# A two-layer transformer block on one core: routed experts as tiles of sorted rows instead of every expert for every token

## The chip, the cores and the metric

The kernel runs on one core of a Trainium2 chip. The metric is the time of one execution on the device, in microseconds (us); less is better. Three runs of the kernel before were taken.

## The reference, cut to what matters

There are 8 batches of 512 tokens with 128 channels. Layer 0 is attention over the heads of a token plus a gated feed-forward of width 384, both on a layer norm of x. Layer 1 normalizes again and adds two branches: a state-space mixer with a scan over the tokens, and a mixture of 8 routed experts, of which each token uses two, plus one shared expert.

```python
xn = _layernorm(x)
x = x + _L0_attn_ref(xn, ...) + _L0_ffn_ref(xn, ...)
xn = _layernorm(x)
x = x + _L1_attn_ref(xn, ...) + _L1_ffn_ref(xn, ...)

# the scan of L1_attn: 256 channels x 16 states, over 512 tokens
hst = dA * hst + dBu;  y = jnp.einsum('bdn,bn->bd', hst, C_t)

# L1_ffn
gates = jax.nn.sigmoid(xf @ Wg)
vals, idx = jax.lax.top_k(gates, 2)
vals = vals / vals.sum(axis=-1, keepdims=True)
shared = jax.nn.silu(xf @ Ws1) * (xf @ Ws3) @ Ws2
h = jax.nn.silu(jnp.einsum('td,edf->tef', xf, We1)) * jnp.einsum('td,edf->tef', xf, We3)
routed = jnp.einsum('tef,efd,te->td', h, We2, w)
out = (shared + routed) / 3
```

## The kernel before, in words

Two blocks follow each other, `layer0` and `layer1`. Every engine has its own instruction stream, written out by hand, and semaphores (objects of the class `Count`) are the only tie between streams. An engine runs its stream in order, so an instruction that waits holds up all that stands behind it. The DRAM tensor `layer0_out` carries x from one block to the other.

**Layer 0** is a loop written out over `b` from 1 to 9. In one turn an engine works on batch `b` (`new`) and finishes batch `b - 1` (`old`). VectorE's stream of one turn is: score products (`score_prod`, L517, four of 128 x 2048), the rotary steps of batch b + 1 (`rope_q`, `rope_k`), sixteen value products (L541), maximum, three `hidden` steps, `statistics` and `normalize` of batch b + 2 (`bn_stats` L474, `bn_aggr` L479, `xn` L489), a reciprocal (L560), and `add_up` (L565), which makes x1 of batch b - 1. GpSimd does the two rest steps of the exponentials (L371, L377) and `root` (L367). SyncE's queue repeats q through DRAM, stacks the parts of the exponentials and stores x1.

**Layer 1** handles one batch in 32 **slots**, `k` from 0 to 31 (`GROUPS`), one for each group of 128 (channel, state) pairs. In the middle, two batches at a time are the body of a loop with registers (`Fori`); the first and the last batch and the tail are written out. In every slot stands the same recurrence over the engines:

- TensorE, `spread_dt` (L1578, tile `p_decay`) waits until the scan of slot k - 2 is done, then `spread_du` (L1583, tile `p_du`) until the `inject` of slot k - 1 is done.
- ScalarE, `decay` (L1178), an exponential in place on `p_decay`.
- VectorE, `inject` (L1421, tile `dbu`), then `scan` of slot k - 1 (L1427, tile `hs`).
- GpSimd, `times_c` of slot k - 1 (L1078, tile `hc`); every fourth slot TensorE sums eight passes of it in `gather_y` (L1592).

```python
pe.wait_ge(scanned.sem, scanned.at(b, k - ND + 1) if k >= ND else scanned.at(b - 1, GROUPS - ND + k + 1))
nc.tensor.matmul(p_decay[:, k % ND], spread[:, i], block_in[:, 0, s, j], start=True, stop=True).then_inc(dt_full.sem, 1)
```

Around this recurrence two other things are placed by slot number. The first is the preparation of the next batch: layer norm and RMS norm (`statistics`, `normalize`, `normalize_rms`), transposes (`turn_x`), `in_proj` (L1540), a convolution of four taps on VectorE (`convolve`, L1328 and L1331), `x_proj`, `dt_proj`, the softplus steps (L1337 to L1346), the split of the result into three bf16 parts (L1351, L1356), and `routing`, 15 small VectorE steps (L1370 to L1403) that rank the gates.

The second is the mixture of experts. It has `UNITS` = 18 **units** per batch, two for each of the eight routed experts and the shared one; the list `unit_slot` gives each unit its slot, from 4 on, and `units(b, p, k, ahead, ...)` yields those that are due. A unit is one half (128 rows) of an expert's hidden width, for all 512 tokens: TensorE `gate` three slots ahead (L1598, tile `p_g`), ScalarE a copy, a tanh and `add_one` (L1185, L1186, L1190), GpSimd `silu` (L1090, tile `sg`), TensorE `up` (L1609, tile `p_u`), VectorE `hidden` (L1440, tile `y_hid`), TensorE `down` (L1616), added up in `p_acc`. For each expert TensorE also spreads its weight per token (`spread_weight`, L1571) and VectorE multiplies x by it (`weigh_x`, L1411, tile `xw`). After slot 31 the next batch's slots 0 to 7 finish the batch: `skip`, `gate_y`, `out_proj`, `copy_sum`, `turn_back` (L1630), `result` (L1444), store.

## Time and profile before

| | us |
|---|---|
| median of 3 runs | 1463.31 |
| lowest and highest | 1457.02, 1466.71 |
| the profiled execution | 1467.0 |
| its span, first to last instruction | 1465.2 |
| its mean granted TensorE clock | 0.877 |

The 1.8 us between the profiled execution and its span lie around the instructions. In the rows below, a line of the timeline has: start, duration, engine, line, operation, output <- inputs, shape, number of instructions merged, and in brackets the idle time before it and what ended it. PEld is the weight load of TensorE. A row of a group of instructions has: busy time and mean ns of one, then the idle time before them. A row of the table of stretches has: the stretch, its length, busy us (and count) of PE, PEld, DVE, ACT and POOL, the granted TensorE clock (1.0 is 2.4 GHz, 0.5 is 1.2 GHz), the DMA share and GB/s. The stretches are cut at the `skip` of slot 3 of each batch, so that one is 32 slots.

### The profile page before, as it was taken

The numbers are of one execution on the slowest core, as the hardware profiler recorded it, in microseconds if no ns is written. First come the engines' busy times: TensorE is split into PE (matmuls) and PEld (weight loads), VectorE is DVE, ScalarE is ACT, GpSimd is POOL, SyncE is SP. The second block draws the span as 40 slices with busy tenths as digits, with TensorE's granted clock in tenths as the row PEclk, the third lists the DMA queues.
The fourth block names the chain that finished last, engine by engine and source line by source line (L and its number), as shares of the span: only waits on it lengthen the run. The fifth ranks groups of instructions, "written<-read, shape, count | busy, mean of one in ns | idle before, by whom it ended". The sixth has DMA issues, their size and how long they took to land. (4 is left out here: it accounts for less than half of the span.)

```text
span 1465.2 us, 14015 instructions
## 1 busy us (share of the span) xinstructions
PE 1113.0 (76%) x3424; PEld 381.1 (26%) x3424; DVE 1122.3 (77%) x1580; ACT 652.6 (45%) x1016; POOL 682.0 (47%) x505
## 2 busy tenths in 40 slices
PE   4577878778755677877887876888787778777887
PEld 1122222222211222322232222223223222222222
DVE  3557777777633778887987988799788798989776
ACT  1111222122214556547555654655755565474543
POOL 0100111011100546655855865576586477558665
PEclk8568987888975789989999998999999899899999
DMA  5983466535100100010110100011010000101100
GB/s 145 259 187 82 113 144 137 124 90 124 29 28 19 41 13 21 22 29 17 22 31 23 22 16 22 16 29 29 16 22 23 24 19 17 29 16 22 29 1 8
DMA packets 52744, 75.38 MB, mean 51 GB/s; under 512 B 7687, under 2 KB 44488, under 8 KB 48064
## 3 DMA queue, kind: packets, MB, share of 16 engines
q1 hardware_dynamic: 52672, 74.64, 21.3%
q14 instruction: 53, 0.43, 0.1%
q8 instruction: 19, 0.31, 0.1%
HBM read 48.92 MB, written 6.82 MB: 38 GB/s over the span
## 5 line engine op out<-in xcount | busy, mean ns | idle before, releaser
L1078 POOL TENSOR_TENSOR hc<-hs,c_rep 128x512 f32<-128x512 f32 x256 | 350.0, 1368 | 320.2 <-DVE hs L1427 318.7
L1178 ACT ACTIVATE p_decay<-p_decay,a_neg 128x512 f32<-128x512 f32 x256 | 169.5, 662 | 320.5 <-PE p_decay L1578 320.2
L1427 DVE TENSOR_TENSOR_SCAN hs<-p_decay,dbu 128x512 f32<-128x512 f32 x256 | 309.7, 1210 | 0.0
L1421 DVE TENSOR_TENSOR dbu<-p_du,b_rep 128x512 f32<-128x512 f32 x256 | 175.5, 686 | 90.9 <-PE p_du L1583 86.6
L1578 PE MATMUL p_decay<-block_in,spread 96*128 96x512 bf16 x256 | 103.7, 405 | 157.9 <-DVE hs L1427 137.4
L1090 POOL TENSOR_TENSOR sg<-sg,g_in 128x512 f32<-128x512 f32 x144 | 205.5, 1427 | 11.5 <-ACT sg L1190 11.5
L1609 PE MATMUL p_u<-xw,w 128*128 128x512 f32 x288 | 177.2, 701 | 38.7 <-DVE xw L1411 37.4
L1598 PE MATMUL p_g<-y_xt,w 128*128 128x512 f32 x288 | 164.4, 654 | 0.0
L1616 PE MATMUL p_acc<-y_hid,w 128*128 128x512 f32 x288 | 160.6, 641 | 4.0 <-DVE y_hid L1440 4.0
L371 POOL TENSOR_TENSOR ex_rest<-ex,ex_part 128x1024 f32<-128x1024 f32 x8 | 17.0, 2128 | 276.5 <-ACT ex_part L422 276.5
L1440 DVE TENSOR_TENSOR y_hid<-p_u,sg 128x512 f32<-128x512 f32 x144 | 98.0, 681 | 58.1 <-issue 51.0
L1185 ACT ACTIVATE g_in<-p_g 128x512 f32<-128x512 f32 x144 | 85.9, 597 | 81.8 <-PE p_g L1598 81.8
L541 DVE TENSOR_TENSOR value_prod<-p_eb,v 128x512 f32<-128x512 f32 x128 | 83.7, 683 | 42.7 <-PE p_eb L694 42.2
L1578 PEld LDWEIGHTS p_decay<-block_in,spread 96*128 96x128 bf16 x256 | 25.6, 100 | 336.6 <-DVE hs L1427 273.2
L1583 PE MATMUL p_du<-block_in,spread 96*128 96x512 bf16 x256 | 102.3, 400 | 0.0
L1190 ACT ACTIVATE sg<-sg 128x512 f32<-128x512 f32 x144 | 90.2, 626 | 0.0
L517 DVE TENSOR_TENSOR score_prod<-qb,p_k 128x2048 f32<-128x2048 f32 x32 | 72.0, 2280 | 20.3 <-PE p_s L658 7.4
L1186 ACT ACTIVATE sg<-p_g 128x512 f32<-128x512 f32 x144 | 85.3, 592 | 0.0
L1609 PEld LDWEIGHTS p_u<-xw,w 128*128 128x128 f32 x288 | 54.3, 210 | 99.1 <-DVE xw L1411 44.6
L1616 PEld LDWEIGHTS p_acc<-y_hid,w 128*128 128x128 f32 x288 | 56.5, 207 | 79.3 <-issue 64.1
L1592 PE MATMUL p_y<-hc,gather 128*32 128x512 f32 x512 | 73.9, 652 | 0.0
L411 ACT ACTIVATE sc<-p_s 128x512 f32<-128x512 f32 x16 | 9.6, 597 | 137.1 <-PE p_s L658 137.1
(163 smaller groups left out, 1578.0 us busy)
## 6 DMA issues: line engine op xcount, KB each, us to landing
qb<-rq_rows SPq DMA_DIRECT2D x32, 1024.0 KB, 13.9
block_in<-y_part SPq DMA_DIRECT2D x192, 64.0 KB, 2.0
stack<-ex_part SPq DMA_DIRECT2D x96, 64.0 KB, 2.1
w<-in_w SPq DMA_DIRECT2D x3, 1152.0 KB, 12.8
y_x<-layer_out SPq DMA_DIRECT2D x9, 256.0 KB, 2.8
x<-in_x SPq DMA_DIRECT2D x8, 256.0 KB, 3.1
rq_rows<-rq SPq DMA_DIRECT2D x8, 256.0 KB, 2.0
layer_out<-x SPq DMA_DIRECT2D x8, 256.0 KB, 2.4
```

What stands on the lines that cost most here:

```text
L1078: nc.gpsimd.tensor_tensor(hc[:, k % NA], hs[:, k % 4], c_rep[:, p], ALU.mult).then_inc(hc_done.sem, 1)
L1090: nc.gpsimd.tensor_tensor(sg[:, m % NG], sg[:, m % NG], g_in[:, m % NG], ALU.mult).then_inc(silu_done.sem, 1)
L1178: nc.scalar.activation(p_decay[:, k % ND], p_decay[:, k % ND], ACT.Exp, scale=a_neg[:, g:g + 1]).then_inc(da_done.sem, 1)
L1190: nc.scalar.activation(sg[:, m % NG], sg[:, m % NG], ACT.Copy, bias=1.0).then_inc(one_more.sem, 1)
L1421: nc.vector.tensor_tensor(dbu[:, k % 4], p_du[:], b_rep[:, p], ALU.mult).then_inc(dbu_done.sem, 1)
L1427: nc.vector.tensor_tensor_scan(hs[:, k % 4], p_decay[:, k % ND], dbu[:, k % 4], 0.0, ALU.mult, ALU.add)\
L1440: nc.vector.tensor_tensor(hid[:, m % 2], p_u[:], sg[:, m % NG], ALU.mult).then_inc(hid_done.sem, 1)
L1578: nc.tensor.matmul(p_decay[:, k % ND], spread[:, i], block_in[:, 0, s, j], start=True, stop=True).then_inc(dt_full.sem, 1)
L1583: nc.tensor.matmul(p_du[:], spread[:, i], block_in[:, 1, s, j], start=True, stop=True).then_inc(du_full.sem, 1)
L1598: nc.tensor.matmul(p_g[:], w1[:, e, bass.ts(f, 128)], xt[:, p], start=True, stop=True).then_inc(g_full.sem, 1)
L1609: nc.tensor.matmul(p_u[:], w3[:, e, bass.ts(f, 128)], xw[:, e % 3], start=True, stop=True).then_inc(u_full.sem, 1)
L1616: nc.tensor.matmul(p_acc[:], w2[:, e, f], hid[:, m % 2], start=(m == 0), stop=False).then_inc(hid_used.sem, 1)
```

## The change

Routing moves from layer 1 into layer 0, and layer 1 computes routed experts only on rows that were sorted by expert. Four batches form a **group**. Layer 0 now also normalizes x1 of batch b - 2 (`pre_statistics`, `pre_normalize`), transposes both normalized forms, computes the gate logits, and stores x plus its norm, and the two transposed forms, in DRAM (`moe["xr"]`, `moe["xt"]`, `moe["ht"]`). After batch 4 and batch 8 VectorE chooses two experts per token (`choose`), TensorE counts (`ranks`), and VectorE turns the counts into a row number per token and choice (`place`). GpSimd sends every token's 129 numbers (128 channels and the weight) to that row of a DRAM table of 24 x 256 rows with indirect DMAs, 128 rows each: the 32 of group 0 in turns 7 and 8 of layer 0, the 32 of group 1 in batch 1 of layer 1, one per slot. SyncE clears the table beforehand.

In layer 1 a routed unit is a **tile** of 256 rows and the whole hidden width of 256, with the weights of the tile's expert fetched by a register: 24 tiles per group, seven per batch in batches 1 to 6, six in batch 7, none in batch 8. With the two units of the shared expert that makes 9, 8 and 2 units per batch. Results are scaled by the row's weight on ScalarE, stored in a DRAM table, and added to x by indirect DMAs with an add, 32 in batch 5 (one per slot) and 32 in batch 8. The convolution becomes four accumulating matmuls with weights scaled by tap. There is no `Fori` any more. TensorE matmuls stay f32.

```diff
-UNITS = (E + 1) * FT1
+GT = 4 * TT
+NTILE = 4 * T * 2 // 256 + E
+TILES = 7
...
+            def pre_statistics(b):
+                dve.wait_ge(x1_done.sem, x1_done.at(b))
+                dve.wait_ge(pre_root.sem, pre_root.at(b - 1))
+                for t in range(TT):
+                    ins = nc.vector.bn_stats(stats[:, t], x1[:, b % 2, t])
...
+            def pre_normalize(b):
+                dve.wait_ge(pre_root.sem, pre_root.at(b))
+                nc.vector.tensor_tensor(rr[:], root2[:, 0], root2[:, 1], ALU.mult).then_inc(pre_done.sem, 1)
+                for t in range(TT):
+                    ins = nc.vector.tensor_scalar(rows[:, TT * (b - 1) + t, 0:D], x1[:, b % 2, t], mv2[:, t, 0:1], root2[:, 0, t:t + 1],
+                                                  ALU.subtract, ALU.mult)
...
                 if new:
                     score_products(b, 0)
+                if pre:
+                    pre_statistics(b - 2)
+                if new:
                     score_products(b, 1)
+                if pre:
+                    pre_normalize(b - 2)
...
+                if b == 7:
+                    place(0)
...
+                if b == 6:
+                    choose(0)
+            choose(1)
+            place(1)
...
+            def send(grp, kk):
...
+                for t in range(GT):
+                    nc.gpsimd.indirect_dma_start(moe["rows"][grp], bass.IndirectOffsetOnAxis(ap=position[:, grp, kk, t:t + 1], axis=0),
+                                                 rows[:, GT * grp + t], None).then_inc(sent[kk], 16)
...
-        unit_slot = [UNIT_LAG + m * GROUPS // UNITS for m in range(UNITS)]
+        plan = []
+        for b in range(1, B + 1):
+            for m in range(FT1 + TILES):
+                tile = TILES * (b - 1) + m - FT1 if m >= FT1 else None
+                if tile is None or tile < 2 * NTILE:
+                    plan.append((GROUPS * (b - 1) + 6 + m * GROUPS // (FT1 + TILES), b, m, tile, len(plan) + 1))
...
+            def load_tile(j, v):
...
+                sp.dma_start(xg[:, r], moe["rows"][grp][256 * i:256 * i + 256].rearrange("(s p) c -> p s c", p=128)).then_inc(xg_in[r].sem, 16)
+                expert = sp.value_load(tile_expert[0:1, grp, i:i + 1], min_val=0, max_val=E)
+                sp.dma_start(wm[:, r], io["wmoe"][bass.ds(expert, 1)].rearrange("o p c -> p (o c)")).then_inc(wm_in[r].sem, 16)
...
+            def half(v):
+                dve.wait_ge(g_read.sem, g_read.at(v))
+                dve.wait_ge(u_full.sem, u_full.at(v))
+                dve.wait_ge(down_done.sem, down_done.at(v - 2))
+                nc.vector.scalar_tensor_tensor(hid[:, v % 2], sg[:, v % 2], 1.0, p_u[:], ALU.add, ALU.mult).then_inc(half_done.sem, 1)
...
+            def project_u(b, n, taps):
...
+                for k in taps:
+                    ins = nc.tensor.matmul(p_misc[:], wtap[:, k, bass.ts(n, 128)], ht[:, b % 2, k:k + T], start=(k == 0), stop=(k == CONV - 1))
...
                     for c, m, j, v in due(b, k, 4):
+                        if j is not None:
+                            turn_tile(v, j)
+                    for c, m, j, v in due(b, k, 3):
+                        gate(v, c, m, j)
                     if nxt:
+                        if 1 <= k <= 4:
+                            project_u(b + 1, (k - 1) // 2, ((0, 1), (2, 3))[(k - 1) % 2])
...
+                    if b == 1:
+                        send(k // GT, k % GT)
+                    if (b, k) in bring:
+                        fetch(*bring[b, k])
```

In units of a tile, `gate` and `up` are two matmuls each of 256 columns and `down` four of 128 columns (tiles `xgt`, `wm`, `p_g`, `p_u`), preceded by two transposes (`turn_tile`). ScalarE copies the transposed rows (`copy_xg`), copies and takes the tanh of `p_g`, and scales the result (`weigh`). GpSimd's product (`hidden`, tile `y_hid`) stays one instruction of 128 x 512 per unit.

Where the instructions stand, at three places. First VectorE in a turn of layer 0, from the end of the turn before; the kernel before:

```order
L489 TENSOR_SCALAR xn<-x,mv,rstd 128x128 x4
L565 TENSOR_TENSOR x<-p_acc,x 128x512
L517 TENSOR_TENSOR score_prod<-qb,p_k 128x2048 x2
L495 SCALAR_TENSOR_TENSOR turn<-p_a,bq,rope 128x512
L497 SCALAR_TENSOR_TENSOR p_a<-p_a,bq,rope 128x512
```

and the changed one (`slots` are the rows to be sent, `xnr` the second norm):

```order
L655 TENSOR_TENSOR score_prod<-qb,p_k 128x2048
L711 BN_STATS stats<-x 128x6 x4
L717 BN_AGGR mv<-stats 128x2 x4
L720 TENSOR_SCALAR var<-mv 128x4
L723 RECIPROCAL rr<-var 128x4
L725 TENSOR_TENSOR rr<-rr,mv 128x4
L727 TENSOR_SCALAR var<-rr 128x4
L655 TENSOR_TENSOR score_prod<-qb,p_k 128x2048
L731 TENSOR_TENSOR rr<-root 128x4
L733 TENSOR_SCALAR slots<-x,mv,root 128x128 x4
L739 TENSOR_SCALAR xnr<-x,mv,rr 128x128 x4
L633 SCALAR_TENSOR_TENSOR turn<-p_a,bq,rope 128x512
```

Six rows of statistics now stand between the first two score products and three rows of norms behind the second, ahead of the rotary steps. Second, TensorE in layer 1, slot 9 of a batch in the middle (`y_misc` is the tile that `p_misc` names), before:

```order
L1578 MATMUL p_decay<-block_in,spread 128x512
L1582 REGISTER_ALU
L1583 MATMUL p_du<-block_in,spread 128x512
L1571 MATMUL p_u<-wt,pick 128x512
L1597 REGISTER_ALU
L1598 MATMUL p_g<-y_xt,w 128x512
L1524 REGISTER_ALU
L1540 MATMUL y_misc<-y_ht,win 128x512
L1606 REGISTER_ALU
L1609 MATMUL p_u<-xw,w 128x512
```

and changed:

```order
L1773 MATMUL p_decay<-block_in,spread 128x512
L1778 MATMUL p_du<-block_in,spread 128x512
L1794 MATMUL p_g<-ident,xg 128x128 x2
L1754 MATMUL y_misc<-y_ht,win 128x512
L1829 MATMUL p_acc<-y_hid,shared_w 128x512
```

Besides the projection of the next batch the slot held two 512-column steps of units and a weight spread; now it holds one such step and two small transposes, and no register arithmetic. Third, GpSimd in batch 1 of layer 1, before:

```order
L1078 TENSOR_TENSOR hc<-hs,c_rep 128x512
L1090 TENSOR_TENSOR sg<-sg,g_in 128x512
L1078 TENSOR_TENSOR hc<-hs,c_rep 128x512
L1066 TENSOR_TENSOR dtu<-dtu 128x512
L1070 TENSOR_TENSOR dtu<-dtu,u 128x512
```

and changed (`moe_rows` is the table in DRAM, `position` the row numbers):

```order
L1408 TENSOR_TENSOR hc<-hs,c_rep 128x512
L1420 TENSOR_TENSOR y_hid<-y_hid,g_in 128x512
L1396 TENSOR_TENSOR dtu<-dtu 128x512
L1400 TENSOR_TENSOR dtu<-dtu,u 128x512
L1428 DMA moe_rows<-slots,position 6144x129
```

An indirect DMA now stands in each slot of batch 1; in batches 5 and 8 it is one that adds rows to `y_xr`.

## Rows read from the trace of the kernel before

**Rows 1.** The page's head: span, and busy time by engine

```profile
span 1465.2 us, 14015 instructions
...
PE 1113.0 (76%) x3424; PEld 381.1 (26%) x3424; DVE 1122.3 (77%) x1580; ACT 652.6 (45%) x1016; POOL 682.0 (47%) x505
```

**Rows 2.** Table of stretches: layer 0, the start of layer 1, two batches

```profile
130.00:423.00 293.00, 233.81 (x890) 76.06 (x888) 209.43 (x284) 65.63 (x83) 29.60 (x16) 0.86 0.44 103
423.00:487.00 64.00, 21.94 (x40) 8.12 (x41) 25.50 (x74) 21.08 (x27) 11.40 (x10) 0.53 0.15 39
...
744.90:868.20 123.30, 97.56 (x289) 34.73 (x288) 106.59 (x147) 70.38 (x113) 80.00 (x59) 0.93 0.10 23
...
1364.50:1457.00 92.50, 78.60 (x237) 25.84 (x237) 71.62 (x90) 46.89 (x79) 63.26 (x50) 0.96 0.05 12
```

**Rows 3.** Timeline of layer 1, one slot of batch 8

```profile
1417.15 0.39 PE L1578 MATMUL p_decay<-block_in,spread 96*128 96x512 bf16 x1 [1.21 <-DVE hs L1427]
...
1417.38 0.38 PE L1583 MATMUL p_du<-block_in,spread 96*128 96x512 bf16 x1
...
1417.86 0.69 DVE L1421 TENSOR_TENSOR dbu<-p_du,b_rep 128x512 f32<-128x512 f32 x1
...
1418.47 1.21 DVE L1427 TENSOR_TENSOR_SCAN hs<-p_decay,dbu 128x512 f32<-128x512 f32 x1
...
1419.60 0.67 DVE L1440 TENSOR_TENSOR y_hid<-p_u,sg 128x512 f32<-128x512 f32 x1
...
1419.74 0.39 PE L1578 MATMUL p_decay<-block_in,spread 96*128 96x512 bf16 x1 [0.27 <-DVE hs L1427]
```

**Rows 4.** Timeline of layer 1, TensorE alone, a slot in a middle batch

```profile
1107.19 1.02 PE L1598 MATMUL p_g<-y_xt,w 128*128 128x512 f32 x2
1108.05 0.60 PE L1533 MATMUL y_misc<-ident,y_xn 128*128 128x128 f32 x4
1108.49 1.02 PE L1616 MATMUL p_acc<-y_hid,w 128*128 128x512 f32 x2
1109.44 1.06 PE L1592 MATMUL p_y<-hc,gather 128*32 128x512 f32 x8
```

**Rows 5.** Groups of instructions on DVE, layer 1

```profile
L1427 DVE TENSOR_TENSOR_SCAN hs<-p_decay,dbu 128x512 f32<-128x512 f32 x256 | 309.7, 1210 | 0.0
L1421 DVE TENSOR_TENSOR dbu<-p_du,b_rep 128x512 f32<-128x512 f32 x256 | 175.5, 686 | 90.9 <-PE p_du L1583 86.6 <-issue 1.9
L1440 DVE TENSOR_TENSOR y_hid<-p_u,sg 128x512 f32<-128x512 f32 x144 | 98.0, 681 | 58.1 <-issue 51.0 <-PE p_u L1609 2.5 <-POOL sg L1090 0.8
...
L1331 DVE SCALAR_TENSOR_TENSOR conv<-ur,vecs,conv 128x512 f32<-128x512 f32 x48 | 50.9, 1060 | 0.7
```

**Rows 6.** Groups of instructions on POOL

```profile
L1078 POOL TENSOR_TENSOR hc<-hs,c_rep 128x512 f32<-128x512 f32 x256 | 350.0, 1368 | 320.2 <-DVE hs L1427 318.7
L1090 POOL TENSOR_TENSOR sg<-sg,g_in 128x512 f32<-128x512 f32 x144 | 205.5, 1427 | 11.5 <-ACT sg L1190 11.5
...
L371 POOL TENSOR_TENSOR ex_rest<-ex,ex_part 128x1024 f32<-128x1024 f32 x8 | 17.0, 2128 | 276.5 <-ACT ex_part L422 276.5
```

**Rows 7.** Timeline of layer 0, end of a turn

```profile
258.92 0.86 DVE L474 BATCH_NORM_STATS2 stats<-x 128x6 f32<-128x128 f32 x4
...
259.94 0.38 DVE L479 BATCH_NORM_AGGREGATE mv<-stats 128x2 f32<-128x6 f32 x4 [0.16 <-DVE stats L474]
...
263.87 1.01 DVE L489 TENSOR_SCALAR xn<-x,mv,rstd 128x128 f32<-128x128 f32 x4
```

**Rows 8.** Timeline between the layers: last add, routing, first decay

```profile
422.95 0.69 DVE L565 TENSOR_TENSOR x<-p_acc,x 128x512 f32<-128x512 f32 x1 [7.22 <-PE p_acc L734]
...
447.91 0.17 DVE L1370 TENSOR_SCALAR gates<-eg 128x32 f32<-128x32 f32 x1
...
452.65 0.19 DVE L1403 TENSOR_TENSOR wpart<-wrest,wpart 128x32 bf16<-128x32 f32 x1
...
485.90 0.61 PE L1578 MATMUL p_decay<-block_in,spread 96*128 96x512 bf16 x1 [18.54 <-DMA block_in<-y_part]
```

1067 lines of the change are left out of this document (608 added, 459 removed).

## The prediction

> **What bounds the kernel now.** I read the head of the page first: VectorE is busy 77% of a span of 1465.2 us and TensorE 76% [rows 1], so neither is full and an average decides nothing. The table of stretches then splits the span. Layer 0 with its start takes 423 us, the start of layer 1 another 63 to 64, and a batch in the middle of layer 1 takes 123.3 us, in which VectorE is busy 106.6, TensorE 97.6, GpSimd 80.0 and ScalarE 70.4; batch 8, which prepares no successor, takes 92.5 [rows 2]. The layer-1 batches are about two thirds of the span, and there the change takes work away.
>
> Next I read one slot on the timeline. `p_decay` starts at 1417.15, `p_du` at 1417.38, the inject at 1417.86, the scan at 1418.47, and the next `p_decay` at 1419.74, just behind the scan [rows 3]. That is a loop: scan, two spreads, inject, scan. It takes 2.59 us a slot even with nothing else in the way, 82.9 us for 32 slots. Two things in it are free: VectorE's gap of about 0.7 us between the scan and the next inject (here a `y_hid` stands in it and costs nothing), and TensorE's time after the spreads, 2.59 - 0.45 = 2.14 us. Whatever a slot holds beyond these lengthens it. The groups of instructions agree: the scan never waits, the inject waited 86.6 us in all for `p_du` [rows 5].
>
> **A slot sum, tried on the kernel before.** For each slot I take the largest of 2.59; 0.45 plus TensorE's other work; and 1.9 plus VectorE's other work. TensorE's prices are start-to-start on the timeline: a 512-column f32 step 0.86 (1107.19 to 1108.05), four transposes 0.44 (1108.05 to 1108.49), a gather of four 1.0 [rows 4]. On VectorE 0.6 for a 512-column product behind another. For a middle batch before this gives 119, measured 123.3; for batch 8 it gives 92, measured 92.5 [rows 2]. It runs about 4 short where the code is the register loop.
>
> **Layer 1, what goes.** Per middle batch TensorE loses the 18 old units (18 x 3 x 0.86 = 46 us), eight weight spreads, the transposes of the norm and the logits. VectorE loses, net, nine `hidden`, nine `weigh_x`, the taps (six of 1.06 [rows 5] and two shorter), 15 routing steps and the norms, some 34 us of 106.6. GpSimd loses nine products of 1.43 [rows 6], ScalarE all 18 `add_one`.
>
> **Layer 1, what comes.** A tile costs TensorE 0.22 for two transposes, 0.86 for gate, 0.86 for up (half the columns, twice the matmuls) and for down eight passes of 128 columns. No row shows that shape with its weight load; by columns it is 0.86, by the loads and transposes of 128 columns (0.11 each and more) up to 1.8. I take 1.3, the middle; both ends move a batch by less than 2 us, because a down mostly fits in the free 2.14. The four taps per half are eight matmuls, 6.9 us, in slots 1 to 4, in place of 1.7. ScalarE, at 70.4 of 123.3 us before, only loses on balance and is no bound. The slot sum is then 82.9, plus 6.7 where TensorE overfills a slot (1 to 4: taps beside unit steps, 3.2; slot 6: 1.2; slot 14, `x_proj`: 1.4; 16 and 30: 0.9), plus 5.1 where VectorE does (softplus in 18, 19 and 21: 3.4; rest steps and result in 7, 8, 24, 26: 1.7): 94.7. I add 2 for new waits (`up` on `weigh` of the tile before, decay behind `weigh` on ScalarE), as the register arithmetic is gone: **97 us** for batches 2, 3, 4 and 6, 96 for batch 7.
>
> The loads of tile and weights are issued eight slots ahead, over 20 us; SyncE's waits in between (`stack`, `repeat_bc`, `store_tile`) hold it up for a slot or two, so they stay hidden. If that cover were gone each tile would wait for its load, some 2 to 3 us.
>
> **GpSimd's indirect DMAs.** Batches 1, 5 and 8 hold one per slot, and each stands in the stream before the next `times_c`; behind `times_c` wait the scan four slots on and the gather. No row shows what an indirect DMA holds GpSimd. From below zero is out, since GpSimd's issue is added work: 0. From above I take its longest instruction, 2.13 [rows 6]. The nearest row is an instruction that handles all 128 partitions once, `hc` with 1.37 [rows 6]; I take 1.35. GpSimd then has 80.0 - 9 x 1.43 = 67 us per batch at most [rows 2, 6], plus 32 x 1.35 = 43: 110 in batches 1 and 5, above 97, so there it is the bound. Batch 8: 63.3 - 16 x 1.43 = 40, plus 43 = 83, beside a slot floor of 83 and little more; 88. GpSimd sets the time in batches 1 and 5 from 0.94 us per DMA on.
>
> The Trainium skill, "DMA: Bandwidth & Descriptors", Specifications, puts the first byte of a DMA issued from GpSimd at about 1 us; taken as the hold, an estimate by that page would make batches 1 and 5 some 99 us and the total about 22 us less. No run here shows it yet.
>
> Layer 1 from the first decay to the end of slot 31 of batch 8: 110 + 3 x 97 + 110 + 97 + 96 + 88 = 792. Before it was 1465.2 - 16 - 485.9 = 963, with 16 for the tail: three slots and the last 8.1 us [rows 2].
>
> **Layer 0, what comes.** In turns 3 to 8 VectorE gains, in its own stream, statistics 0.86 + 0.16 + 0.38 [rows 7], four small steps of about 0.2, and 0.2 + 1.0 + 1.1 for the two norms (1.01 for four [rows 7]): 4.7 us. GpSimd's root hides behind the second score product. Behind these steps stand the rotary steps and everything after; VectorE is busy 209 of 293 us [rows 2] but its waits come later in the turn and are chains from its own results, so I count nothing hidden: 6 x 4.7 = 28. TensorE's transposes and logits stand where it waits for score products. `choose` and `place` of group 0 are 33 small steps; 15 routing steps took 4.9 us from 447.91 to 452.84 [rows 8], 0.29 each, so 9.5. Turn 9 gains 4.7, a bare root and a TensorE chain of transposes, copies and logits, and GpSimd's 16 sends in turn 8 may make its root late: 11. Then a turn 10, all in a chain: statistics, root and norms 6, two transposes with copies 3, logits and exponential 2.5, `choose` until the mask 4.5, counting 2, `place` 3.5: 21. The clears and stores go to queues that are not full here; nothing, at worst 10.
>
> **Between the layers.** From the last add at 422.95 to the first decay at 485.90 are 63 us [rows 8]. The norm and logits leave (some 10), a store and load through DRAM stays, the wider tap weights are loaded and scaled, and eight tap matmuls come at a clock that was 0.53 here [rows 2]: 8 x 1.6 = 13. Net 3 more.
>
> **Sum.** First decay at 485.9 + 28 + 9.5 + 11 + 21 + 3 = 558. Plus 792, plus 16 for the tail and 1 for the last fetches: 1367 of span. The profiled execution of before lies 1.8 above its span: **1369 us**. It was itself 1467.0 where the median of the runs was 1463.3, 0.3% less, which I leave in the range.
>
> **Rivals.**
> A, the other side: GpSimd becomes the bound so far that all is lost. The price is 3 x 32 = 96 DMAs in layer 1 plus some 16 in layer 0 that are not covered, 112 in all. From 1.35 us per DMA, each 0.1 more costs 11 us; the gain of 98 is gone at about 2.2 us. At 2.8 the time would be 1369 + 112 x 1.45 = 1531. For it: each works through a list of 128 rows, and GpSimd's own products of one shape already differ, 1.37 for `hc` and 1.43 for `sg` [rows 6], so it is slowed by its neighbours. Against: no instruction of GpSimd in the trace takes over 2.2 us. The Trainium skill, "SBUF — State Buffer", "SBUF: two separate sides", says that GpSimd cannot write descriptors while VectorE runs a two-port operation on SBUF; by that rule the sends of layer 0 beside the norms would be late, while layer 1 keeps few such operations. The trace has no such DMA and bears neither out.
> B: the batches of layer 1 shrink less, because TensorE's clock falls or the tile's chain (turn, copy, gate, tanh, up, half, product, down, weigh) gets late. TensorE is granted 0.93 there now with a busy share of 0.79, and 0.53 between the layers where it is busy a third of the time [rows 2]; the new share is near 0.68. At a granted clock of 0.85 the 66 us of TensorE work in a batch take 6 longer, and a unit that is late by half a us adds 4 or so: 8 a batch is what I price, 8 x 8 = 64, so 1433.
> C: GpSimd's DMAs are cheap (0.7 us) and slots run at the floor more often (92 a batch): 1369 - 2 x 13 - 5 x 5 - 8 = 1310.
>
> **How the numbers follow.** The forecast has 0.58, A 0.12, B 0.17, C 0.13. The forecast's own range is 1335 to 1410 (2 per batch on the tile's down, 10 on the clears, 15 on the turns). The range reaches into B and C and to the bound of 2.13 us per DMA (1369 + 112 x 0.78 = 1456): 1315 to 1455. About 1% is what a measurement of this kernel can tell from no change. Faster by more: 0.58 + 0.13 + 0.14 of B = 0.85; within 1%: 0.02 of A and 0.02 of B = 0.04; slower 0.11.
>
> **What would show it.** Per batch of layer 1: 97 for batches 2 to 4 and 6, and batches 1 and 5 longer by 13 with the inject or scan waiting for `hc`; a slot without extra work still 2.59; first decay near 558; turns of layer 0 longer by 4.7; the hold of an indirect DMA readable as the gap between two `hc`. I am wrong if batches 2 to 4 differ by more than 8 us from 97, if batch 1 is not longer than batch 2, or if layer 0 grows by over 90.

## The result, and the profile after

The changed kernel takes 1529.55 us (median of 4 runs, 1525.82 to 1531.11) against 1460.78 (4 runs, 1457.02 to 1466.71) for the kernel before on the same chip: the ratio is 1.0463, 95% interval 1.0435 to 1.0492. It is 4.6% slower, where 1369 us was forecast. The profiled execution took 1530.53 us, its span 1528.7.

The page's head beside [rows 1]: every engine has less to do than before, TensorE 1043.5 us against 1113.0, VectorE 931.9 against 1122.3, ScalarE 531.5 against 652.6, only GpSimd 731.5 against 682.0. What was added is waiting.

```profile
span 1528.7 us, 12782 instructions
...
PE 1043.5 (68%) x3556; PEld 434.9 (28%) x3556; DVE 931.9 (61%) x1288; ACT 531.5 (35%) x850; POOL 731.5 (48%) x547
```

The last add of layer 0 and the first decay of layer 1, which answer to [rows 8]:

```profile
475.09 0.69 DVE L704 TENSOR_TENSOR x<-p_acc,x 128x512 f32<-128x512 f32 x1 [5.22 <-PE p_acc L1003]
...
554.15 0.61 PE L1773 MATMUL p_decay<-block_in,spread 96*128 96x512 bf16 x1 [20.64 <-DMA block_in<-y_part]
```

The table of stretches of layer 1, columns as in [rows 2], here cut at the first inject of each batch (batches 1, 4, 5 and 8, and the sum of all eight):

```profile
555.30:675.30 120.00, 82.33 (x278) 39.19 (x278) 72.85 (x80) 54.50 (x92) 90.25 (x75) 0.80 0.27 76
...
913.80:1033.10 119.30, 88.39 (x304) 42.24 (x303) 75.13 (x84) 55.60 (x95) 63.53 (x48) 0.79 0.22 62
1033.10:1165.60 132.50, 90.95 (x304) 43.12 (x303) 79.10 (x83) 55.57 (x95) 114.00 (x79) 0.76 0.34 75
...
1405.50:1512.00 106.50, 56.74 (x146) 11.20 (x146) 67.69 (x72) 25.21 (x39) 95.17 (x68) 0.60 0.21 33
sum 956.70, PE 668.63 PEld 300.11 DVE 594.76 ACT 412.03 POOL 619.90; mean PE 83.58 PEld 37.51 DVE 74.35 ACT 51.50 POOL 77.49
```

A middle batch takes 119.3 us where 97 was forecast, though VectorE (75) and GpSimd (64) were busy for about as long as forecast. TensorE was not: 88.4 us against the 66 of the forecast. Batch 1 took 120.0 and batch 2, which has no indirect DMAs, 118.8, where a difference of 13 was forecast. The first decay stands near its forecast, at 554.15 against 558, and the end of the last batch lies 16.7 us before the end of the span, against 16 + 1. The whole miss of 162 us is in the eight batches: 956.7 against 792.

The waits of the changed kernel (for what, us in total, times, longest):

```profile
DVE dbu L1652 <- PE p_du L1778: 316.2, 195, 8.4
...
ACT os L1543 <- PE p_u L1834: 133.3, 48, 8.6
...
PEld p_u L1834 <- POOL y_hid L1420: 91.4, 48, 8.0
```

The inject waited 86.6 us for `p_du` before [rows 5] and now 316.2. The third row is new in kind: the down of a tile (L1834), the last TensorE step of a unit, waits for GpSimd's product, 48 times, which is every tile. One such slot on the timeline (slot 13 of batch 3):

```profile
838.22 1.27 POOL L1408 TENSOR_TENSOR hc<-hs,c_rep 128x512 f32<-128x512 f32 x1 [1.32 <-DVE hs L1658]
...
838.64 1.03 PE L1807 MATMUL p_g<-xgt,wm 128*128 128x256 f32 x4
...
839.45 1.27 POOL L1420 TENSOR_TENSOR y_hid<-y_hid,g_in 128x512 f32<-128x512 f32 x1
839.52 1.21 DVE L1658 TENSOR_TENSOR_SCAN hs<-p_decay,dbu 128x512 f32<-128x512 f32 x1
...
840.77 2.08 PE L1834 MATMUL p_u<-wm,y_hid 128*128 128x128 f32 x8 [1.10 <-POOL y_hid L1420]
...
842.64 0.63 PE L1773 MATMUL p_decay<-block_in,spread 96*128 96x512 bf16 x1
...
843.80 0.69 DVE L1652 TENSOR_TENSOR dbu<-p_du,b_rep 128x512 f32<-128x512 f32 x1 [3.07 <-PE p_du L1778]
```

GpSimd does `hc` first and the unit's product second, so the product ends at 840.72, 2.5 us after `hc` began. TensorE has been free since 839.67, waits until 840.77, and the down then holds the next two spreads, which could have gone at the end of the scan (840.73), until 842.64. VectorE stands idle for 3.07 us before the inject; before the inject of this slot it was idle 0.77 us.

By slots (from one inject to the next) the slot sum of the forecast was right where the product is not waited for, or hardly (0.4 us in slot 2): slots 0 to 5 of batch 2 took 2.6, 3.3, 3.0, 3.3, 3.9, 2.6 (sum: 2.6, 3.2, 3.5, 3.0, 3.9, 2.6). Slots 6 and 9, each with a down of the shared expert, and 13, 20, 23, 27 and 30, each with a down of a tile, took 5.1, 5.3, 4.5, 4.3, 4.9, 5.5 and 6.9 where it had 3.8, 2.6, 2.6, 2.6, 2.6, 2.6 and 3.1; slot 14 with `x_proj` took 9.3 instead of 4.0.

Three causes had to be told apart. Theory 1: an order of instructions makes the down late. Theory 2: TensorE's granted clock (0.79 in a middle batch, 0.93 before [rows 2]) makes the slots long. Theory 3: the indirect DMAs, by what they hold and whom they slow.

### The profile page after: what moved, and what is told of

Its sections match the earlier page's. It is cut to its first block and busy times, and to the rows that moved or that the text cites. A ratio compares the mean times of both kernels' runs of the same rounds, so it can differ in the third digit from the quotient of the medians.

```text
span 1528.7 us, 12782 instructions
## 1 busy us (share of the span) xinstructions
PE 1043.5 (68%) x3556; PEld 434.9 (28%) x3556; DVE 931.9 (61%) x1288; ACT 531.5 (35%) x850; POOL 731.5 (48%) x547
## 5 line engine op out<-in xcount | busy, mean ns | idle before, releaser
L1652 DVE TENSOR_TENSOR dbu<-p_du,b_rep 128x512 f32<-128x512 f32 x256 | 176.6, 690 | 323.1 <-PE p_du L1778 316.2
L1834 PE MATMUL p_u<-wm,y_hid 128*128 128x128 f32 x384 | 86.6, 396 | 68.1 <-POOL y_hid L1420 68.0
L1778 PE MATMUL p_du<-block_in,spread 96*128 96x512 bf16 x256 | 120.2, 470 | 0.4 <-DVE dbu L1652 0.4
L1444 POOL DMA_INDIRECT y_xr<-moe_sums,position x64 | 105.2, 1644 | 10.0 <-issue 7.9
L1834 PEld LDWEIGHTS p_u<-wm,y_hid 128*128 128x128 f32 x384 | 74.5, 288 | 91.7 <-POOL y_hid L1420 91.4
L1420 POOL TENSOR_TENSOR y_hid<-y_hid,g_in 128x512 f32<-128x512 f32 x64 | 90.7, 1417 | 0.0
L1543 ACT ACTIVATE os<-p_u,xg 128x128 f32<-128x128 f32 x96 | 30.1, 364 | 133.3 <-PE p_u L1834 133.3
L1744 PE MATMUL y_misc<-y_ht,wtap 128*128 128x512 f32 x128 | 64.1, 627 | 15.3 <-DVE a_neg L1621 14.4
L923 PE MATMUL p_s<-score_prod,sum_d 128*32 128x512 f32 x256 | 52.7, 909 | 31.6 <-DVE score_prod L655 31.5
L1671 DVE SCALAR_TENSOR_TENSOR y_hid<-sg,p_u 128x512 f32<-128x512 f32 x64 | 43.0, 673 | 45.8 <-issue 45.7
L1807 PE MATMUL p_g<-xgt,wm 128*128 128x256 f32 x192 | 68.6, 494 | 0.0
L1820 PE MATMUL p_u<-xgt,wm 128*128 128x256 f32 x192 | 67.3, 485 | 0.0
```

The lines of the kernel that those rows point to most:

```text
L1420: nc.gpsimd.tensor_tensor(hid[:, v % 2], hid[:, v % 2], g_in[:, v % 2], ALU.mult).then_inc(hid_done.sem, 1)
L1444: nc.gpsimd.indirect_dma_start(xr[:, b - 1, t], None, moe["sums"][grp], bass.IndirectOffsetOnAxis(ap=position[:, grp, kk, TT * i + t:TT * ...
L1652: nc.vector.tensor_tensor(dbu[:, k % 4], p_du[:], b_rep[:, p], ALU.mult).then_inc(dbu_done.sem, 1)
L1778: nc.tensor.matmul(p_du[:], spread[:, i], block_in[:, 1, s, j], start=True, stop=True).then_inc(du_full.sem, 1)
L1834: ins = nc.tensor.matmul(p_u[:, bass.ts(i, 128)], hid[:, v % 2, 256 * f + 128 * i:256 * f + 128 * i + 128], wm[:, j % NR, 2 * FF1 + 128 * ...
```

## The experiments

**e1_swap**, GpSimd's product ahead of `hc`:

```diff
+                    for _, _, _, v in due(b, k, 1):
+                        hidden(v)
                     if old and k == 0:
                         times_c(b - 1, q, GROUPS - 1)
                     if new and k:
                         times_c(b, p, k - 1)
-                    for _, _, _, v in due(b, k, 1):
-                        hidden(v)
```

> One change against the changed kernel: in GpSimd's stream the product of a unit (y_hid) stands ahead of the slot's hc product instead of behind it. Theory 1 (the down of a unit finds its product unfinished and holds the next two spreads behind it on TensorE): the seven tile downs of a middle batch, in slots 6, 13, 16, 20, 23, 27 and 30, and slot 9 end 1.1 to 2 us earlier each, slot 14 up to 2 more because the silu behind weigh comes earlier; a middle batch falls from 119.7 us to 100 to 106, the total from 1530 to 1390 to 1430, and the time in which the inject waits for p_du falls from 316 us to under 180. Theory 2 (TensorE's lower granted clock, 0.79 against 0.93, is what lengthens the slots, the waits follow from it): the middle batch falls by at most 4 us, the total stays above 1495. Theory 3 (the indirect DMAs and what they do to their neighbours): a middle batch, which has none, stays at 119 to 120.

Measured: 1442.83 us (4 runs), ratio to before 0.9869 (0.9835 to 0.9902), so 87 us less than the changed kernel. Middle batches 103.7 to 107.9. The wait of the down for `y_hid` falls from 91.4 to 19.2 us, ten times instead of 48, and the inject's wait for `p_du` to 220.9; theory 1 had said under 180, and a total of 1390 to 1430. The clock rose with it, from 0.79 in batches 2 to 4 to 0.85, 0.92 and 0.83. The same slot of batch 3:

```profile
808.48 1.26 POOL L1420 TENSOR_TENSOR y_hid<-y_hid,g_in 128x512 f32<-128x512 f32 x1
...
809.84 1.26 POOL L1408 TENSOR_TENSOR hc<-hs,c_rep 128x512 f32<-128x512 f32 x1
...
810.43 1.91 PE L1807 MATMUL p_g<-xgt,wm 128*128 128x256 f32 x4
...
812.13 1.71 PE L1834 MATMUL p_u<-wm,y_hid 128*128 128x128 f32 x8
...
813.68 0.38 PE L1773 MATMUL p_decay<-block_in,spread 96*128 96x512 bf16 x1
```

The product is done before the slot begins and TensorE goes from gate to down without a wait. `hc`, now later, costs next to nothing: TensorE's gathers waited 22.0 us for it in layer 1 of the changed kernel and 23.2 us here. Theory 1 has its main part; theory 2 alone (above 1495) and theory 3 for a middle batch (119) are out.

**e2_nodma**, the 96 indirect DMAs of layer 1 and the waits on them taken out:

```diff
-                    if b == 1:
-                        send(k // GT, k % GT)
-                    if (b, k) in bring:
-                        fetch(*bring[b, k])
```

> Leaves out the 96 indirect DMAs of layer 1 (the 32 sends of batch 1 and the 64 fetches with add of batches 5 and 8), so the routed rows of the second group and all routed results are missing from the output. Theory 3 (the indirect DMAs are what is lost): batches 1, 5 and 8 fall from 129.9, 132.3 and 102.4 us to about 118, 118 and 88, the last 2 us of the tail go, and the middle batches fall as well if SyncE's own DMAs were slowed: total near 1490 or below. Theory 1: only 10 to 12 us each of batches 1, 5 and 8, 30 to 38 in all, since GpSimd has slack elsewhere: total 1492 to 1500, middle batches unchanged at 119 to 120.

Measured: 1494.49 us (one run), 35 less. Batches 1, 5 and 8 (first inject to last) fell from 120.0, 132.6 and 103.5 to 115.4, 119.6 and 99.4; the middle ones stayed at 117.1 to 120.2. The total is the one that theory 1 gave, its parts are not: batch 5 gained 13.0 us, but batches 1 and 8 gained 4.6 and 4.1 and not 10 to 12. And not all of the 35 us comes from the DMAs. The first inject stands at 547.6 here and at 555.3 in the changed kernel, though the edit touches nothing ahead of it; over all kernels of this record it lies between 547.6 and 557.0. Of the rest, 3.7 us are the tail, and 24.7 the eight batches, 956.7 against:

```profile
sum 932.00, PE 662.05 PEld 295.79 DVE 586.23 ACT 412.36 POOL 487.16; mean PE 82.76 PEld 36.97 DVE 73.28 ACT 51.54 POOL 60.89
```

The DMAs are a cause of their own, worth 25 of the 165 us in the batches.

**e3_notile**, no tiles at all (and no indirect DMA):

```diff
-            for m in range(FT1 + TILES):
+            for m in range(FT1):
```

> Leaves out the routed tiles (all their loads, matmuls, activations and products) and the 96 indirect DMAs of layer 1; the two units of the shared expert per batch and the preparation of the next batch stay. It measures what a middle batch costs without tiles. By the slot sum of the prediction a batch is 82.9 us plus taps, projections and softplus: 92 to 94. Theory 1 says that nearly all of the 120 us above it is the tiles' waits, so the middle batch is 92 to 97 us. Theory 2 says that at a still lower granted clock (0.6 to 0.7) the slots with taps, x_proj and gather stay long: 103 or more.

Measured: 1421.19 us (one run), a middle batch 106.2 or 108.8 us, with a granted clock of 0.69 or 0.65, and 0.59 in batch 8. That is theory 2's figure: most slots took 3.0 us instead of 2.6. So less work on TensorE does not mean a shorter slot. Slot 6 still took 7.7 us: the shared unit's down has the same order and waits 1.02 us for its product, and the down, a gather and the transposes back take 2.08, 1.94 and 1.12 us at the low clock.

**e4_downshape**, the down as two matmuls of 256 columns:

```diff
-                        ins = nc.tensor.matmul(p_u[:, bass.ts(i, 128)], hid[:, v % 2, 256 * f + 128 * i:256 * f + 128 * i + 128],
-                                               wm[:, j % NR, 2 * FF1 + 128 * f:2 * FF1 + 128 * f + 128], start=(f == 0), stop=(f == FT1 - 1))
+                    ins = nc.tensor.matmul(p_u[:, 0:256], wm[:, j % NR, 2 * FF1 + 128 * f:2 * FF1 + 128 * f + 128],
+                                           hid[:, v % 2, 256 * f:256 * f + 256], start=(f == 0), stop=(f == FT1 - 1))
```

> The down of a tile is written as two accumulating matmuls of 256 columns with the weights held in the array, instead of four of 128 columns with the hidden rows held; the amount of work is the same, the result comes out transposed, so the routed rows of the output are other numbers. A tile down took 2.08 us in the slots where it stood behind the wait. If theory 1 holds, each down stands on the path once its product is late, and the whole of what the shape saves (2.08 to 1.9 or 1.0) shortens its slot: middle batch 119.7 to 112 to 119. If down were covered, as the prediction had it, nothing changes: 119 to 120.

Measured: 1522.44 us (one run), middle batches 116.3 to 119.9. The down's time on TensorE did not change (86.2 us in all, 86.6 in the changed kernel), only its weight loads (49.5 us against 74.5). The shape was no cause. As the down's time did not change, the run does not say what a shorter down would have given.

**e5_silu**, on top of e1_swap, ScalarE's silu one slot earlier:

```diff
-                    if k == 13:
+                    if k == 12:
                         silu_u_z(b + 1, q)
```

> On top of e1_swap: ScalarE's three silu of the next batch stand in slot 12 instead of 13. In e1_swap slot 14 of a middle batch took 8.2 to 8.7 us, where the slot sum had 4.0: TensorE waited 2.4 us for the silu, and x_proj then took 3.4 us at the low clock. Theory 1a (the order of ScalarE's stream is the cause): the wait of x_proj goes, slot 14 falls to 5 to 6.5 us, seven times: total 1443 to 1422 to 1430. Theory 1b (the table load and silu delay the decay just as much one slot earlier): slots 12 and 13 grow by what 14 loses, total within 5 us of 1443.

Measured: 1413.14 us (4 runs), ratio 0.969 (0.9663 to 0.9717): 30 less than e1, more than expected. Slot 14 took 4.1 us in four of seven batches and 4.6 to 5.3 in the others, and slots behind it got shorter too, with a higher granted clock. Batches 3 to 6:

```profile
763.90:862.80 98.90, 72.96 (x304) 35.49 (x303) 74.59 (x84) 55.29 (x95) 63.98 (x48) 0.93 0.27 74
862.80:961.70 98.90, 72.97 (x304) 35.52 (x303) 74.58 (x83) 55.26 (x95) 63.99 (x48) 0.93 0.28 74
961.70:1087.60 125.90, 89.79 (x304) 43.18 (x303) 85.00 (x84) 55.83 (x95) 114.01 (x79) 0.77 0.36 79
1087.60:1189.30 101.70, 74.59 (x303) 36.00 (x302) 74.71 (x83) 55.21 (x95) 65.51 (x49) 0.92 0.30 78
```

A middle batch is now 98 to 99 us, the forecast's 97, at a granted clock of 0.93 again. Same work, no added filling: the low clock of the changed kernel was for the larger part a consequence of its waits. The two edits moved instructions and added none, and the clock of batch 4 went from 0.79 to 0.83 (e1) and 0.93 (here).

**e12_siluonly**, the silu alone on the changed kernel:

> The changed kernel with ScalarE's silu in slot 12 instead of 13 and nothing else, so without the swap of e1. On top of the swap this gave 30 us (1443 to 1413), seven batches. If the two causes are independent: 1530 to 1500, slot 14 from 8.6 to 9.3 down to 4.5 to 5.5. If the late product still holds x_proj's slot (the down of slot 13 ends late, everything in TensorE's stream behind it too): 1510 to 1522, slot 14 at 6 to 8.

Measured: 1509.18 us (one run), just under the second figure: 20 less. Slot 14 fell to 4.1 to 5.6, as in the first. The two orders do not quite add up: 87 and 20 alone, 116 together.

**e6_warm**, on top of e1_swap, the gate and up matmuls of tiles (as in the line below) and the shared unit's gate issued twice:

```diff
-                for f in range(FT1):
+                for f in (0, 1, 0, 1):
```

> On top of e1_swap: every gate and every up matmul is issued twice, with the same result; about 15 us of TensorE work more per middle batch, most of it in the free 2.14 us of its slot. Theory 2 (the slots are long because the clock fell): the granted clock goes from 0.79 towards 0.9 and the total falls by 5 to 25 us, though there is more work. Theory 1 (waits and order, the clock a small matter): slots 6, 13, 20 and 27, which hold a gate and a down, and slot 14 grow by 0.9 each, 4 to 5 us a batch: total 1465 to 1480.

Measured: 1454.55 us (10 runs, 1451.12 to 1469.52), ratio 0.9965 (0.9933 to 0.9998): 12 slower than e1, between the figures of the two theories. The granted clock rose from 0.794 to 0.836, and it did not pay: slots 3, 6 and 10 grew by 0.6 to 0.9.

**e9_fill**, on top of e3_notile, one matmul more in slots 10 to 31:

```diff
+                    if new and k >= 10:
+                        if k == 10:
+                            pe.wait_ge(g_read.sem, g_read.at(FT1 * b))
+                        nc.tensor.matmul(p_g[:], shared[:, 0:128], shared[:, 0:512], start=True, stop=True)
```

> On top of e3_notile (which leaves out the routed tiles and the indirect DMAs of layer 1): in slots 10 to 31 of every batch TensorE does one matmul of 512 columns more, into p_g, which nobody reads; 22 x 0.86 us of work added per batch. In e3_notile those slots took 3.0 us at a granted clock of 0.6 to 0.69. Theory 2: the clock rises and these slots fall from 3.0 to 2.6 us, a middle batch from 106 to 108 to 97 to 100, the total from 1421 to 1350 to 1375. Without the clock at work the added matmul is hidden at best: slots stay at 3.0, total 1421, or longer if it takes 1.7 us and pushes the next spreads.

Measured: 1397.77 us (one run), 23 less with more work. Theory 2 had said 1350 to 1375. The clock rose from 0.69 to 0.84 in batch 4 and from 0.59 to 0.87 in batch 8. Batch 8 fell from 99.4 to 91.3 us, its empty slots from 3.0 to 2.6. The middle batches gained only 0.4 to 3 us: what slots 10 to 21 won, slots 22, 26 and 30 lost, where the added matmul stood beside a gather. Theory 2 is real, at 0.4 us a slot without work, 8 us in batch 8; it is not the 22 us of a middle batch.

**e7_spread**, on top of e1_swap, the DMAs of batches 1 and 5 in every second slot of two batches:

```diff
-                    if b == 1:
-                        send(k // GT, k % GT)
+                    if b in (1, 2) and k % 2 == 0:
+                        at = (GROUPS * (b - 1) + k) // 2
+                        send(at // GT, at % GT)
```

> On top of e1_swap: the 32 sends of batch 1 stand in every second slot of batches 1 and 2, and the first 32 fetches in every second slot of batches 5 and 6; the fetches of batch 8 stay. Theory 3 (GpSimd's stream is full where one indirect DMA stands in each slot: 93 to 112 us of 105 to 130): batch 5 falls from 127 to 107 to 110 and batch 6 rises by 1 to 4, batch 1 falls from 111 to 105: total 1443 to 1418 to 1426. Rival (each fetch costs its time wherever it stands, through the neighbours that it slows): what batch 5 loses batch 6 gains, total 1437 to 1443.

Measured: 1448.12 us (4 runs), ratio 0.9923 (0.99 to 0.9947): no gain. Batch 5 fell to 115.8 and batch 6 rose to 116.2, together 232.0, as in e1 (127.2 + 105.0 = 232.2). The rival was right for this placing. But the lost time stood in few slots: 6, 21, 24 and 26. The timeline of slot 24 of batch 6 tells why:

```profile
1180.51 1.58 POOL L1445 DMA_INDIRECT y_xr<-moe_sums,position  x1
1181.51 3.11 POOL L1409 TENSOR_TENSOR hc<-hs,c_rep 128x512 f32<-128x512 f32 x2
1181.55 5.37 DVE L1642 TENSOR_TENSOR conv<-dtu,y_part 128x1024 f32<-128x1024 f32 x1
...
1186.84 0.68 DVE L1654 TENSOR_TENSOR dbu<-p_du,b_rep 128x512 f32<-128x512 f32 x1
```

A VectorE step with both inputs in SBUF took 5.37 us; in a batch without indirect DMAs the same step takes 1.20. The inject stands behind it.

**e10_quiet**, on top of e5_silu, no DMA in the slots of those steps:

```diff
+        quiet = [k for k in range(GROUPS) if k < 5 or 9 <= k < 17 or k >= 27]
+        last = [k for k in range(GROUPS) if k < 5 or k >= 10] + [12, 16, 20, 24, 28]
```

> On top of e5_silu: the indirect DMAs stand in slots 0 to 4, 9 to 16 and 27 to 31 alone, where VectorE has no step of 1024 elements with both inputs in SBUF (softplus and rest steps, slots 6, 8, 18 to 26): the sends in batches 1 and 2, the first fetches in batches 5 and 6, those of batch 8 in slots 0 to 4 and 10 to 31, five of them two to a slot. In e7_spread such a VectorE step took 3.2 to 5.4 us beside a DMA instead of 1.2, and a fetch 2.38 instead of 1.57. Theory 3b (GpSimd's descriptor work and these VectorE steps hold each other up, a DMA elsewhere is nearly free): batch 1 falls from 108.9 to 99 to 102, batch 5 from 125.8 to 100 to 105, batch 6 stays within 3 of 101.8, batch 8 falls from 103.4 to 96 to 100; total 1413 to 1372 to 1388. Rival (each DMA costs its 0.7 us wherever it stands, as e7_spread against e1_swap has it): batches 1 and 2 together stay at 207, batches 5 and 6 at 227, total 1408 to 1415.

Measured: 1400.33 us (5 runs), ratio 0.9603 (0.9565 to 0.9641): 13 less, half of what was expected or under. Slots 21 to 26 of batch 5 were cured (batch 5 from 125.8 to 109.0, batch 1 from 108.9 to 95.6). Batches 2, 6 and 8, to which DMAs were moved or in which they were doubled, took more: 103.8, 106.1 and 105.9 where they had taken 98.1, 101.8 and 103.4. Slot 6 was not cured, 8.7 us, and in batch 8 10.4, though the last fetch stands two slots ahead of it in the stream. In time it does not:

```profile
963.60 1.57 POOL L1449 DMA_INDIRECT y_xr<-moe_sums,position  x1 [0.16 <-issue]
...
964.62 1.85 POOL L1425 TENSOR_TENSOR y_hid<-y_hid,g_in 128x512 f32<-128x512 f32 x1
965.06 4.94 DVE L1645 TENSOR_TENSOR conv<-dtu,y_part 128x1024 f32<-128x1024 f32 x1
...
966.53 2.08 PE L1834 MATMUL p_acc<-y_hid,shared_w 128*128 128x512 f32 x2 [2.45 <-POOL y_hid L1425]
...
971.31 0.40 PE L1778 MATMUL p_decay<-block_in,spread 96*128 96x512 bf16 x1
...
972.03 0.69 DVE L1657 TENSOR_TENSOR dbu<-p_du,b_rep 128x512 f32<-128x512 f32 x1 [2.04 <-PE p_du L1783]
```

A fetch and an `hc` took 3.03 us together (fetches at 957.53, 960.57 and 963.60), more than a slot's 2.59, so GpSimd fell behind; the fetch of slot 4 ran in slot 6. Two things then stood in that slot: the unit's product was late, so that the down waited 2.45 us (4.99 in batch 8), and VectorE's step took 4.94 us, from 0.1 us before the fetch's end on. The late product ended last: VectorE was free again 2.04 us before the inject and waited for `p_du`, whose spread stood on TensorE behind the late down, a gather and the transposes back. The step alone would have held the inject until about 970.0, which makes a slot of 6.7 us (an estimate from these rows).

**e11_fill8**, on top of it, the filling matmul in slots 11 to 31 of batch 8:

> On top of e10_quiet: in slots 11 to 31 of batch 8, where TensorE has only two spreads and a gather every fourth slot, it does one matmul of 512 columns more, into p_g, which nobody reads. Theory 2 (at the lower clock a spread takes 0.63 us instead of 0.39, so an empty slot takes 3.0 us instead of 2.6): the 21 slots fall by 0.3 to 0.4 each, batch 8 by 6 to 8 us. If GpSimd's DMA and product are the bound of these slots (1.57 + 1.27 = 2.84): by 2 to 3 us. If the added work only costs: batch 8 is longer.

Measured: 1402.29 us (4 runs), ratio 0.9603 (0.9559 to 0.9648), the same as e10. The clock in batch 8 rose to 0.80 and slots fell to 2.6, until GpSimd was behind with `hc`; slot 22, where the gather waited 3.42 us for it, then took 8.5 (5.7 in e10). So the time won came back at once, and GpSimd's stream of fetches and `hc` is the bound of these slots.

**e13_quieter**, no DMA in slots 3 and 4 either:

```diff
-        quiet = [k for k in range(GROUPS) if k < 5 or 9 <= k < 17 or k >= 27]
-        last = [k for k in range(GROUPS) if k < 5 or k >= 10] + [12, 16, 20, 24, 28]
+        quiet = [k for k in range(GROUPS) if k < 3 or 9 <= k < 17 or k >= 27]
+        last = [k for k in range(GROUPS) if k < 3 or k >= 9] + [GROUPS + k for k in (0, 1, 3, 4, 5, 6)]
```

> On top of e10_quiet: no indirect DMA in slots 3 and 4 either (0 to 2, 9 to 16 and 27 to 31 in batches 1, 2, 5 and 6; 0 to 2 and 9 to 31 in batch 8, none doubled, the last six in slots 0, 1, 3, 4, 5 and 6 behind it). In e10_quiet slot 6 of batches 5, 6 and 8 still took 8.7, 8.9 and 10.4 us against 3.7 in a batch without, though the last fetch stood two slots ahead; the VectorE step in it took 4.94 us. Theory 3c (the descriptor work of a fetch runs on behind the instruction and is late by several slots when they stand in a row; VectorE's step waits for all of it): slot 6 falls to 3.7 to 5, batches 5 and 6 by 3 to 5 each, batch 8 from 105.9 to 94 to 99, the tail grows by 0 to 5; total 1400 to 1384 to 1392. Rival (slot 6 is long for another reason of these batches, the load of SyncE's queue or the result of the batch): slot 6 stays above 8, total 1396 to 1404.

Measured: 1380.89 us (4 runs), ratio 0.9472 (0.9435 to 0.9509): the best version, 5.3% faster than before and 149 us faster than the change as it was made. Slot 6 took 3.7 us in batches 5 and 6 and 5.2 in batch 8. In batch 5 the down no longer waits and the step is back at its length:

```profile
963.93 1.02 PE L1834 MATMUL p_acc<-y_hid,shared_w 128*128 128x512 f32 x2
...
965.08 1.20 DVE L1645 TENSOR_TENSOR conv<-dtu,y_part 128x1024 f32<-128x1024 f32 x1
```

Both causes of e10's slot 6 left together, so this run does not say how much was each. Not all was cured: in batch 6 a step in slot 18, 2.2 us behind the start of a fetch, took 3.64 us instead of 1.40, and the slot 5.9 instead of 3.6. The tail grew from 16.2 us (e5) to 23.5. The sum of its eight batches is 799.0 us, where the forecast was 792:

```profile
sum 799.00, PE 567.84 PEld 258.92 DVE 586.01 ACT 410.27 POOL 611.54; mean PE 70.98 PEld 32.37 DVE 73.25 ACT 51.28 POOL 76.44
```

The tail gives the price of a fetch on GpSimd by itself. Back to back, two start 1.86 us apart:

```profile
1362.86 1.55 POOL L1449 DMA_INDIRECT y_xr<-moe_sums,position  x1 [0.16 <-issue]
1364.72 1.55 POOL L1449 DMA_INDIRECT y_xr<-moe_sums,position  x1 [0.30 <-issue]
```

**e14_floor**, e5_silu without indirect DMAs in layer 1 and with the filling in batch 8:

> e5_silu without the 96 indirect DMAs of layer 1 (left out: the sends of the second group and all fetches, so no routed result reaches the output) and with the filling matmuls of e11 in slots 11 to 31 of batch 8. It tests whether order and DMAs together are all that lay between forecast and result. By the forecast's slot sum, without DMAs: seven batches of 97 and one of 88 from the first decay at 555, and 16 behind: span 1338. If order, DMAs and the clock in batch 8 are all: batches 1 to 7 at 96 to 102, batch 8 at 91 to 94, span 1345 to 1365. If something else is left: a batch above 104, or a span above 1370.

Measured: 1346.61 us (one run), span 1344.7, eight batches 784.0. By the bounds set for it nothing large is left: batch 2, at 102.7, is the only one above its range. The first inject stands at 548.4 here, 7 us earlier than in the changed kernel, behind a layer 0 that is the same in both; without that the span would be 1352. The indirect DMAs weigh more once the other waits are gone: batches 1 to 7 took 731.4 us with them (e5) and 692.2 without, 39.2 less, where e2 gave 20.6 for the same seven. So the shares of the causes depend on the order in which they are taken away. Batches 2 and 4 of e14 hold the same instructions and differ by the clock:

```profile
642.90:745.60 102.70, 77.53 (x304) 38.73 (x303) 75.15 (x84) 55.45 (x95) 64.07 (x48) 0.88 0.26 72
...
846.70:943.20 96.50, 70.16 (x304) 34.20 (x303) 74.47 (x83) 55.20 (x95) 63.97 (x48) 0.96 0.28 76
```

Slots 14, 16, 27 and 30 make most of the difference; whether a wait or the clock came first in batch 2 is not shown.

## Why the prediction was wrong

The miss in the batches, 956.7 against 792, is taken apart by the runs, sums of eight batches: the swap gives back 85.5 (to 871.2), the silu 33.5 (to 837.7), the placing of the DMAs 38.7 (to 799.0, with 7 us given back in the tail). What is left is 7. Taken in another order the shares differ: the silu alone gives 21.0 (e12), the DMAs left out first 24.7 (e2).

- **"I add 2 for new waits": the step that failed.** The forecast priced the tile's chain by durations alone and named `up` on `weigh` and decay behind `weigh`. The chain's last link on GpSimd was passed over: the order on GpSimd, where `hidden` stands behind `times_c`, so that the product was ready only after TensorE wanted it, for each of the 48 tiles and 91.4 us in all. With the fall of the clock that came with it, this cost 14.4 us in a batch without DMAs (119.5 against 105.1 on average) and 85.5 over all eight, where the term held 2 a batch. In the kernel before, GpSimd's part (`silu`) came ahead of VectorE's, with slots between it and the down, so the trace showed no such wait. The order stood in the streams and could have been read there.
- **"slot 14, `x_proj`: 1.4".** The kernel before already took 5.5 us in that slot. The sum had priced the work in the slot (4.0 in all) and no wait. Here ScalarE had `weigh`, which waits for the late down of slot 13, ahead of the silu, and the slot took 9.3; with the silu a slot earlier it took 4.1. The whole effect was 33.5 us over seven batches, part of it the clock.
- **The slot sum, 82.9 + 6.7 + 5.1 = 94.7: right for the high clock.** With the orders mended and without DMAs, batches 4 and 6 took 96.5 at a clock of 0.96; batches 2, 3, 5 and 7 took 99.3 to 102.7 at 0.88 to 0.93 (e14). The sum had no term for the clock.
- **TensorE's 66 us of work in a batch.** It was 70.2 at a clock of 0.96 (e14) and 88.4 at 0.79 in the changed kernel.
- **"I take 1.3" for a tile's down: right for the high clock.** 48 downs took 63.7 us in e13, 1.33 each, and 86.6 us in the changed kernel, 1.80 each, which is the upper bound. That a down "mostly fits in the free 2.14" was not true while it was late. No run made the down itself shorter, so that "both ends move a batch by less than 2 us" is not shown; e4, which changed only its weight loads, gave about 1 us a batch.
- **Batch 8, 88 by forecast.** It took 106.5. Without DMAs and with a filled TensorE it is 91.8. The larger price that was missing is the clock: empty slots take 3.0 us at 0.60, with fetches or without (e2: 102.4). The other is slot 6, 10.5 us with the DMAs and 5.4 without (e2). That a fetch with an `hc` takes 3.03 us shows only once the slots are shorter than that (e11).
- **An indirect DMA, 1.35 us (bounds 0 to 2.13).** A send held GpSimd 0.98 to 1.14 us by its rows, a fetch 1.76 (3.03 less the 1.27 of an `hc`) to 1.86. The value lay between, within the bounds. "GpSimd sets the time in batches 1 and 5" was not so in batch 1: busy 90.25 of 120.0 us, the batch is 1.2 longer than batch 2 and not 13, and 4.6 shorter without its sends (e2). In batch 5 GpSimd was busy 114.0 of 132.5 us, and without the fetches the batch took 13 less. There it did set the time of single slots, by falling behind: in slot 27 (10.2 us, 4.7 without DMAs) a down waited 7.62 us for a product that stood behind two fetches and two `hc`.

```profile
1147.45 2.08 PE L1834 MATMUL p_u<-wm,y_hid 128*128 128x128 f32 x8 [7.62 <-POOL y_hid L1420]
```

- **Rival A's rule.** It had the SBUF port in view for layer 0 and said that "layer 1 keeps few such operations". There are six slots with two-input steps in a batch, and it was VectorE that was hurt, not only the DMA: 1.20 us became up to 5.4. The Trainium skill, "SBUF — State Buffer", "SBUF: two separate sides", counts a VectorE operation with two SBUF inputs among those that contend with a GpSimd operation that reads SBUF, and says that the one that comes second "fully blocks" for the other's instruction. Away from DMAs the traces agree, as in e14: a step that began with 0.70 us of an `hc` still to run took 1.78 us instead of 1.20, and the product that GpSimd began during it took 2.26 instead of 1.27.

```profile
727.21 1.27 POOL L1402 TENSOR_TENSOR hc<-hs,c_rep 128x512 f32<-128x512 f32 x1
...
727.78 1.78 DVE L1633 TENSOR_TENSOR y_part<-conv,y_part 128x1024 bf16<-128x1024 f32 x1
...
728.43 2.26 POOL L1414 TENSOR_TENSOR y_hid<-y_hid,g_in 128x512 f32<-128x512 f32 x1
```

  Beside a DMA the rule does not give the size: to be blocked for the whole of the DMA's 1.58 us would make a step of 2.8 us, and it took 5.37 (e7). What holds it so long stays open. Rival A's total, 1531, came out, but by luck and not by A's mechanism: the DMAs are worth 28 us of it (e2, batches and tail), not 162.
- **Rival B** named the right place, "a unit that is late", and the fall of the clock, at 8 us a batch. It was 22. (By its own terms, 6 for the clock and 4 for the late units, the price would have been 10.)
- **Layer 0: right in the sum, by luck in part.** The last add is 52.1 us later (forecast 28 + 9.5 + 11 = 48.5), the first decay 68.3 later (forecast 72). But turns 3 to 9 grew by 62.6 us, from add to add by 7.0, 6.4, 3.0, 7.7, 15.5, 10.0 and 13.0, so 14 more than forecast. Against that the first add, at the end of turn 2, came 10.4 us earlier, a term that the forecast did not have:

```profile
129.55 0.69 DVE L565 TENSOR_TENSOR x<-p_acc,x 128x512 f32<-128x512 f32 x1 [4.39 <-PE p_acc L734]
...
119.11 0.69 DVE L704 TENSOR_TENSOR x<-p_acc,x 128x512 f32<-128x512 f32 x1 [4.40 <-PE p_acc L1003]
```

  Turn 2 gets none of the new steps, and TensorE has 148 matmul records in it either way; it was granted 0.73 in the kernel before and 0.85 here. From the last add to the first decay it took 8 us less than forecast (16.1 more than before, not 21 + 3). A small error is in the price of 0.29 for a small step: the rows from 447.91 to 452.84 are 16 steps of 0.31, which makes 10.2 for 33 steps and not 9.5.
